# Layer 0 of a two-layer kernel: logits, dispatch, combine and first expert products as three f16 products of split halves, with a new order of steps

## The reference

```python
xn = rmsnorm(x, norm_gamma)
sn = rmsnorm(slot_embeds, slot_norm_gamma)
logits = jnp.einsum('bnd,esd->bnes', xn, sn)
dispatch = jax.nn.softmax(logits, axis=1)
combine = jax.nn.softmax(logits.reshape(b, n, e * s), axis=-1)
slots = jnp.einsum('bnd,bnes->besd', xn, dispatch)
h = jnp.einsum('besd,edh->besh', slots, w1) + b1[None, :, None, :]
h = jax.nn.gelu(h, approximate=False)
eo = jnp.einsum('besh,ehd->besd', h, w2) + b2[None, :, None, :]
out = jnp.einsum('bmd,bnm->bnd', eo, combine)
```

## Time and profile before

| | |
|---|---|
| median of 3 runs | 3189.1 us |
| lowest and highest run | 3177.04 and 3196.51 us |
| the profiled execution | 3176.99 us |
| its span, first to last instruction | 3175.3 us |
| mean granted clock of TensorE, share of full speed | 0.987 |
| PE busy in the span | 2998.4 us (94%) |
| PE weight loads | 1597.1 us (50%) |
| DVE busy | 2243.0 us (71%) |
| ACT busy | 1765.3 us (56%) |
| POOL busy | 1316.9 us (41%) |

### The profile page before, as it was taken

The page is one execution under the profiler, slowest core; times in us unless marked ns, Lnnn a source line. Parts: engine busy times, 40 slices in busy tenths (PEclk is TensorE's granted clock), DMA queues, the critical chain, the costliest instruction groups (busy, mean ns, idle before and its releaser), DMA issues.

```text
span 3175.3 us, 62002 instructions
## 1 busy us (share of the span) xinstructions
PE 2998.4 (94%) x22724; PEld 1597.1 (50%) x22724; DVE 2243.0 (71%) x4069; ACT 1765.3 (56%) x3674; POOL 1316.9 (41%) x1223
## 2 busy tenths in 40 slices
PE   4999999999999995799999999999999999999997
PEld 2565555555555553344444444444444444444443
DVE  4666666666666663787787787778778778878774
ACT  2666666665566664555555555555555555555543
POOL 1333333333333331354545545545544554455453
PEclk9999999999999998899999999999999999999998
DMA  4222222222222222434444445444444444453442
GB/s 119 51 53 51 51 51 56 64 56 63 51 51 51 62 50 83 110 100 117 128 113 123 116 115 135 111 112 126 115 121 112 128 126 104 125 135 100 124 121 67
DMA packets 271901, 297.58 MB, mean 94 GB/s; under 512 B 30832, under 2 KB 235760, under 8 KB 271088
## 3 DMA queue, kind: packets, MB, share of 16 engines
q1 hardware_dynamic: 249936, 276.88, 34.2%
q10 hardware_dynamic: 21664, 16.73, 1.7%
HBM read 141.46 MB, written 25.69 MB: 53 GB/s over the span
## 4 chain that ended last, share of the span: by engine, by line
PE 50%; DMA 3%; DVE 3%; issue 2%; SPq 2%; ACT 1%; POOL 0%; DVEq 0%; ACTq 0%; POOLq 0%
PE l_ps_out L1569 8%; PE l_ps_any L1469 6%; PE l_ps_any L1471 6%; PE l_ps_any L1470 6%; PE l_ps_any L1594 5%; PE l_ps_exp L1552 4%; PE l_ps_exp L1554 4%; PE l_ps_any L1601 4%; PE l_ps_any L1527 3%; DMA l_y_rec<-rec_scratch 2%; PE l_ps_sum L1580 2%; PE l_ps_exp L1556 2%; SPq L1099 1%; DVE l_neg_max L1392 1%; PE l_ps_any L1532 1%
## 5 line engine op out<-in xcount | busy, mean ns | idle before, releaser
L614 DVE TENSOR_REDUCE neg_max<-ps_any 128x1 f32<-128x384 f32 (+3 forms) x704 | 417.7, 636 | 264.0 <-PE ps_any L728 259.5
L1186 POOL TENSOR_TENSOR l_hid<-l_hid,l_spread 128x512 f32<-128x512 f32 x256 | 328.3, 1282 | 652.0 <-DVE l_hid L1421 481.1
L1273 ACT ACTIVATE l_probs<-l_ps_exp 128x512 f32<-128x512 f32 x640 | 376.8, 595 | 212.3 <-PE l_ps_exp L1556 201.8
L501 ACT ACTIVATE probs<-ps_exp 128x512 f32<-128x512 f32 x640 | 349.2, 602 | 151.5 <-PE ps_exp L743 150.8
L442 POOL TENSOR_SCALAR_AFFINE_SELECT probs<-probs 128x512 f32<-128x512 f32 x256 | 160.0, 637 | 591.1 <-ACT probs L501 591.1
L1392 DVE TENSOR_REDUCE l_neg_max<-l_ps_any 128x2 f32<-128x768 f32 (+2 forms) x384 | 316.3, 863 | 36.1 <-PE l_ps_any L1532 35.1
L1552 PE MATMUL l_ps_exp<-l_q_a,l_k_a 128*128 128x512 f16 (+3 forms) x1024 | 306.4, 300 | 10.0 <-DMA l_q_b<-l_max_row 6.3
L1569 PE MATMUL l_ps_out<-l_probs,l_v 128*64 128x512 f32 (+3 forms) x2048 | 303.9, 439 | 0.7 <-ACT l_yT L1248 0.7
L1425 DVE TENSOR_TENSOR l_hw<-l_hid,l_hw 128x512 f16<-128x512 f32 x272 | 258.6, 955 | 59.4 <-ACT l_hw L1256 58.9
L1554 PE MATMUL l_ps_exp<-l_q_b,l_k_b 65*128 65x512 f16 (+3 forms) x1024 | 295.3, 300 | 0.0
L1279 ACT ACTIVATE l_hid<-l_ps_any 128x512 f32<-128x512 f32 x272 | 162.4, 597 | 234.8 <-PE l_ps_any L1471 217.5
(11 more groups left out here) (233 smaller groups left out, 6514.4 us busy)
## 6 DMA issues: line engine op xcount, KB each, us to landing
l_spread<-route_scratch SPq DMA_DIRECT2D x128, 512.0 KB, 4.7
l_q_a<-l_q_hi SPq DMA_DIRECT2D x256, 128.0 KB, 2.4
l_y_rec<-rec_scratch SPq DMA_DIRECT2D x128, 256.0 KB, 4.3
l_q_b<-l_q_lo SPq DMA_DIRECT2D x128, 128.0 KB, 2.4
l_k_a<-l_k_hi SPq DMA_DIRECT2D x128, 128.0 KB, 3.0
l_k_a<-l_k_lo SPq DMA_DIRECT2D x128, 128.0 KB, 2.7
l_k_b<-l_k_hi SPq DMA_DIRECT2D x128, 128.0 KB, 2.7
q_st<-rot_hi SPq DMA_DIRECT2D x64, 128.0 KB
```

Of the source, the lines that this page charges most:

```text
L501: nc.scalar.activation(probs[:, n % 2, u], ps_exp[:, (10 * g + u) % 3], ACT.Exp, scale=float(HD0 + DR) ** -0.5).then_inc(exp_done.sem, 1)
L614: nc.vector.tensor_reduce(neg_max[:, n % 2, heads[0]:heads[0] + k, t], src, AX.X, ALU.max, negate=True).then_inc(drained["dve"], 1)
L1186: nc.gpsimd.tensor_tensor(at, at, spread[:, c % 3, n % SPREAD], ALU.mult).then_inc(weighted.sem, 1)
L1273: nc.scalar.activation(probs[:, n % 2, u], ps_exp[:, (5 * p + u) % ST_BANKS], ACT.Exp, scale=float(HD1) ** -0.5).then_inc(exp_done.sem, 1)
```

## The change

- `snT`, `xfT`, `xf` (as a new tile `xf_p`), `disp_n`/`comb_s`, `slotsT`, `w1` and `eo` become pairs of f16 halves: the high half is the value rounded to f16, the low half what is left of it. Some are scaled by powers of two (w1 by 64, shares by 1024, slots and eo by 16), and the scales are taken out again in the Gelu and in the copy of `out`.
- The products of `logits_s`, `logits_c`, `slots`, `hidden` and the four of `out` are each three f16 products, high x high, high x low and low x high, accumulated in the same bank (`split_product`). w_o's product and `expert_out` stay in float32, and so do all the turns.
- The high halves are made by ACT and the low halves by DVE, which reads the bank and the high half. For `dispatch` and `combine` every bank is now read by both, ACT first, and is free once DVE is done; the same holds for `slots` and `xfT`. `xf`'s halves are made from SBUF, ACT in the step `xf` and DVE in `xfT`. `eo` is first added into `eo_in` by DVE, then ACT makes the high half in the step `expert_out`, and DVE the low half in a new step `eo_lo`.
- w1 is loaded first on ACT's queue, in float32, into the half of `probs` that head group 1 will use, and split at the first `turn_max` by one ACT and one DVE instruction of 4096 columns; ACT waits for DVE's before the first Exp of group 1. `snT` gets its low half from DVE before DVE's first `norm`, and PE waits for it.
- `ORDER0` is another order of the same steps and `eo_lo`. The second and later `logits_s` come later in relation to the attention's groups; `attnT`, `out` and `outT` of a pass stand in the next pass; `dispatch` follows `max` 2_7; `xf` of the next pass comes after the exps of group 3 have begun, and `xfT` after the next pass's `max` 0_10; the `max` steps of the next pass's groups 0 and 1 reach further ahead.

The core of the diff:

```diff
-    ("max", 0, 1, 2), ("max", 0, 1, 3), ("max", 0, 1, 4), ("exp", 0, 0, 3), ("soft_s", 0, 0), ("exp", 0, 0, 4),
...
-    ("exp", 1, 0, 1), ("exp", 1, 0, 2), ("max", 1, 1, 1),
+    ("exp", 0, 0, 4), ("logits_s", 0, 0), ("exp", 0, 0, 5), ("exp", 0, 0, 6), ("soft_s", 0, 0),
+    ("max", 0, 1, 8), ("exp", 0, 0, 7), ("attnT", -1, 0), ("load_heads", 0, 2), ("values", 0, 0, 0),
...
+    ("outT", -1, 0), ("max", 0, 2, 5), ("max", 0, 2, 6), ("exp", 0, 1, 4), ("max", 0, 2, 7), ("dispatch", 0, 0),
+    ("dispatch", 0, 1), ("dispatch", 0, 2), ("norm", 1, 0), ("exp", 0, 1, 5), ("load_heads", 0, 3),
+    ("values", 0, 0, 2), ("out_rows", 0, 0), ("dispatch", 0, 3), ("max", 0, 2, 8), ("exp", 0, 1, 6),
+    ("max", 0, 2, 9), ("exp", 0, 1, 7), ("slots", 0, 0), ("exp", 0, 1, 8), ("logits_c", 0, 0),
+    ("logits_c", 0, 1), ("soft_c", 0, 0), ("exp", 0, 1, 9), ("turn_rows", 0, 0), ("scale", 1, 0),
+    ("max", 0, 2, 10), ("soft_c", 0, 1), ("hidden", 0, 0), ("xnT", 1, 0), ("square", 1, 0), ("values", 0, 1, 0),
+    ("turn_max", 0, 2), ("hidden", 0, 1), ("values", 0, 1, 1), ("hidden", 0, 2), ("max", 0, 3, 0),
...
+    ("soft_c", 0, 3), ("max", 0, 3, 9), ("logits_c", 0, 3), ("exp", 0, 2, 6), ("max", 0, 3, 10),
...
+    ("values", 0, 2, 0), ("r", 1, 0), ("expert_out", 0, 0), ("combine", 0, 0), ("values", 0, 2, 1),
+    ("exp", 0, 3, 0), ("exp", 0, 3, 1), ("combine", 0, 1), ("exp", 0, 3, 2), ("eo_lo", 0, 0),
+    ("values", 0, 2, 2), ("combine", 0, 2), ("out_rows", 0, 2), ("exp", 0, 3, 3), ("exp", 0, 3, 4),
...
 def by_act0(step):
 
-    name, _, n = step[:3]
-    return name in ("xnT", "xfT", "ckv", "v", "slots", "attnT", "out", "soft_s", "soft_c", "hidden", "turn_max") or (
-        name in ("dispatch", "combine") and n % 2 == 0)
+    name = step[0]
+    return name in ("xnT", "ckv", "v", "attnT", "out", "soft_s", "soft_c", "hidden", "turn_max")
...
+        w1_in = probs[:, 1, 0:E0 * HID // T].rearrange("p u t -> p (u t)").rearrange("p (e h) -> p e h", h=HID)
...
+            act.dma_start(w1_in, a["L0_ffn_w1"].rearrange("e d h -> d e h")).then_inc(w1_loaded, 16)
...
+                if name == "turn_max" and b == 0 and n == 0:
+                    act.wait_ge(w1_loaded, 16)
+                    nc.scalar.activation(w1[:, 0], w1_in, ACT.Copy, scale=W1_SCALE).then_inc(w1_hi, 1)
+                if name == "exp" and (b, n) == (0, 1) and which[1] == 0:
+                    act.wait_ge(w1_ok, 1)
...
+                if name == "expert_out":
+                    emptied(act, f"expert_out{b}")
+                    if b:
+                        filling(act, f"out{b - 1}")
+                    nc.scalar.activation(eo[:, 0].rearrange("p m d -> p (m d)"), eo_in[:], ACT.Copy, scale=EO_SCALE
+                                         ).then_inc(eo_hi.sem, 1)
...
+                    nc.scalar.activation(disp_n[:, n, 0], full(act, f"dispatch{b}_{n}"), ACT.Copy, scale=SHARE
+                                         ).then_inc(turned_hi.sem, 1)
...
+            dve.wait_ge(prep_act, 1)
+            nc.vector.tensor_tensor(snT[:, 1], ps_any[:, 0], snT[:, 0], ALU.subtract).then_inc(prep, 1)
+
+            def low_part(bank, parts, scale):
+
+                return nc.vector.scalar_tensor_tensor(out=parts[:, 1], in0=bank, scalar=scale, in1=parts[:, 0],
+                                                      op0=ALU.mult, op1=ALU.subtract)
...
+                if name == "dispatch":
+                    bank = full(dve, f"dispatch{b}_{n}")
+                    dve.wait_ge(turned_hi.sem, turned_hi.at(b, n + 1))
+                    low_part(bank, disp_n[:, n], SHARE).then_inc(drained["dve"], 1)
...
+            def split_product(out, w, x, first=True, last=True):
+
+                pe.matmul(out, w(0), x(0), start=first, stop=False)
+                pe.matmul(out, w(0), x(1), start=False, stop=False)
+                return pe.matmul(out, w(1), x(0), start=False, stop=last)
...
-                            ins = pe.matmul(out[:, c:c + S0], w1[:, e, hb * P:hb * P + P],
-                                            slotsT[:, e * S0:e * S0 + S0], start=True, stop=True)
+                            ins = split_product(out[:, c:c + S0], lambda k: w1[:, k, e, hb * P:hb * P + P],
+                                                lambda k: slotsT[:, k, e * S0:e * S0 + S0])
```

More of the change, by code:

```diff
@@ L41 @@
 RING = 4
+W1_SCALE = 64.0
+SHARE = 1024.0
+SLOT_SCALE = 16.0
+EO_SCALE = 16.0
 ST_BANKS = 2
@@ L136 @@
[L136 to L145, removed]
@@ L151 @@
[L151 to L160, removed]
@@ L163 @@
+    ("turn_max", 1, 0), ("turn_rows", 0, 3), ("max", 1, 1, 0), ("max", 1, 1, 1), ("max", 1, 1, 2),
+    ("combine", 0, 3), ("exp", 1, 0, 0), ("exp", 1, 0, 1), ("max", 1, 1, 3), ("exp", 1, 0, 2), ("max", 1, 1, 4),
+    ("max", 1, 1, 5), ("max", 1, 1, 6), ("exp", 1, 0, 3), ("max", 1, 1, 7),
 )
@@ L523, in _ @@
                         filling(act, f"out{b - 1}")
-                    copy(f"attnT{b}", attnT[:])
+                    copy(f"attnT{b}", attnT[:], SHARE * EO_SCALE)
                 if name == "out":
@@ L527, in _ @@
                         filling(act, f"outT{b - 1}")
-                    copy(f"out{b}", outT[:])
+                    copy(f"out{b}", outT[:], 1.0 / (SHARE * EO_SCALE))
                 if name == "outT":
@@ L586, in _ @@
                                                        op0=ALU.mult, op1=ALU.mult).then_inc(xf_ok.sem, 1)
+                if name == "turn_max" and b == 0 and n == 0:
+                    dve.wait_ge(w1_hi, 1)
+                    nc.vector.scalar_tensor_tensor(out=w1[:, 1], in0=w1_in, scalar=W1_SCALE, in1=w1[:, 0], op0=ALU.mult,
+                                                   op1=ALU.subtract).then_inc(w1_ok, 1)
+                if name == "xfT":
+                    dve.wait_ge(xf_hi.sem, xf_hi.at(b, 2))
+                    nc.vector.tensor_tensor(xf_p[:, 1], xf[:], xf_p[:, 0], ALU.subtract).then_inc(xf_lo.sem, 1)
+                    low_part(full(dve, f"xfT{b}"), xfT, 1.0).then_inc(drained["dve"], 1)
+                if name == "slots":
+                    bank = full(dve, f"slots{b}")
+                    dve.wait_ge(slots_hi.sem, slots_hi.at(b, 1))
+                    low_part(bank, slotsT, SLOT_SCALE / SHARE).then_inc(drained["dve"], 1)
+                if name == "eo_lo":
+                    dve.wait_ge(eo_hi.sem, eo_hi.at(b, 1))
+                    low_part(eo_in[:], eo[:].rearrange("p c m d -> p c (m d)"), EO_SCALE).then_inc(eo_ok.sem, 1)
                 if name in ("low_q", "low_k"):
@@ L667, in _ @@
             pe.wait_ge(prep_act, 1)
+            pe.wait_ge(prep, 15)
             def bank(name):
@@ L765, in _ @@
                     emptied(pe, f"xfT{b}")
-                    product(f"logits_s{b}_{n}", snT[:, n * P:n * P + P], xfT[:])
+                    split_product(bank(f"logits_s{b}_{n}"), lambda c: snT[:, c, n * P:n * P + P], xfT_part).then_inc(filled, 1)
                 if name == "logits_c":
                     emptied(pe, f"xfT{b}")
-                    product(f"logits_c{b}_{n}", xfT[:, n * P:n * P + P], snT[:])
+                    split_product(bank(f"logits_c{b}_{n}"), lambda c: xfT[:, c, n * P:n * P + P], snT_part).then_inc(filled, 1)
                 if name == "dispatch":
@@ L810, in _ @@
                     out = bank(f"out{b}")
-                    emptied(pe, f"expert_out{b}")
+                    pe.wait_ge(eo_ok.sem, eo_ok.at(b, 1))
                     for c in range(4):
                         emptied(pe, f"combine{b}_{c}")
-                        pe.matmul(out, eo[:, c], comb_s[:, c], start=(c == 0), stop=False)
+                        split_product(out, lambda k: eo[:, k, c], lambda k: comb_s[:, c, k], c == 0, False)
                     emptied(pe, f"attnT{b}")
```

104 lines of the change are left out of this document (65 added, 39 removed).

## The result

| | before | after |
|---|---|---|
| median | 3189.6 us | 3096.5 us |
| lowest to highest | 3177.0 to 3196.5 | 3095.6 to 3103.9 |
| span of the profiled execution | 3175.3 | 3094.8 |
| one pass of layer 0 | 73.9 | 68.3 |

The ratio is 0.9723 with a 95% interval of 0.9705 to 0.9741: 88 us faster by the ratio, 93 by the medians. The two profiled executions lie 80.5 us apart; that of before is the fastest of its runs. Where its other runs spend the 12 us more no trace shows. The time falls inside the range, 6.5 us above the number given.

What follows compares the result with a forecast made beforehand. PE's stream was taken to bound layer 0's sixteen passes: 7.8 us off PE less 1.5 of new waits, 16 x (7.8 - 1.5) - 8.7 = 92 us off, giving 3090 us, range 3050 to 3138.

Steps and rivals of the forecast that it cites:

- The bound is PE's stream: Layer 0's passes: PE, busy 934 of 960 us, sets their length; staying so had chance 0.70, gain 50 to 130 us.
- 3.4 us for the 16 large products: Logits, slots and out: 16 products per pass, each 0.215 us shorter on PE when split than in float32.
- 4.4 us for the small ones: Experts' first products: four `hidden` steps per pass, each 0.70 us instead of 1.79 on PE.
- the routing row: Layer 1's routing product, f16 with a 128x128 load per matmul, 0.025 us each; basis for 0.029 us in `hidden`.
- rival 3: Weight loads pace the 24 small products of a `hidden` step: 17 us slower at worst, 44 faster by half overlap; chance 0.06.
- ACT + 3.6 and DVE + 5.5 us: Added work per pass for making halves: six ACT copies of 0.60 us, eight more DVE low halves of 0.69 us.
- New waits of 1.5 us: PE's added waiting per pass, for banks emptied by two engines and full engines around `hidden`; between 0 and 4 us.
- The 1.0 us for held banks: Ten more bank fillings per pass emptied by ACT then DVE, charged at 0.10 us each.
- the 0.5 us for two full engines around `hidden`: First dispatch to last combine logits: PE down to 23.5 us, ACT up to 24.1, charged 0.5 us per pass.
- rival 4: PE waits for every turned bank: 13 us per pass, 92 us slower, deciding from 7.2 us per pass; chance 0.05.
- The start, 8.7 us: Once: 2.7 us for snT's low half before the statistics, 6 us for splitting w1; bounds 4 and 13.
- The signs: Adds 66 to 69 us apart, `hidden` 0.7, slot logits 0.215, PE above 95%, statistics near 30, then a 6 us gap.

Runs made afterwards that it cites:

- hidden_f32: The changed kernel with only the experts' first products back in float32, w1 and slotsT not split: 3145.8 us, ratio 0.9868, a pass of 71.48 us.
- bank_free: The changed kernel with dispatch and combine banks free after ACT's copy, DVE reading a tile in SBUF instead: 3097.0 us, a pass of 68.37 us.
- no_table: The changed kernel with Exp in the place of Gelu, so that two table loads per pass fall away: 3097.9 us, a pass of 68.20 us.
- old_order: The changed kernel with the order of steps of the kernel before, eo_lo put in behind group 3's third exp: 3205.7 us, ratio 1.0052.

## Why the prediction was right or wrong, point by point

- **The bound is PE's stream: right.** Work put on PE lengthens the pass by 0.7 (hidden_f32) to 1.2 times its time; the table loads taken off ACT give nothing, work taken off DVE a quarter to 0.4.
- **3.4 us for the 16 large products, 4.4 us for the small ones: right as PE time.** 0.217 and 0.029 us by the rows of after; the routing row was the right neighbour, and rival 3 is out. The Trainium skill's "TensorE: Matmul & The Clock Gate", section "LDWEIGHTS (loading the stationary operand)", gives a load as its columns over 1.2, some 107 ns for 128 columns. The trace agrees with that as a duration (0.098 us for the loads of `hidden`) and not as a pace (0.029 us).
- **ACT + 3.6 and DVE + 5.5 us: a bit high.** 48.0 and 51.0 us per pass are 1.9 and 4.1 more. Records that follow one another overlap, by 0.17 us in DVE's row of eight maxima at 68.00 us ((4.33 - 0.69)/7 = 0.52 us apart), which the sum counted twice. That could cover DVE's 1.4 us, and only a part of ACT's 1.7.
- **New waits of 1.5 us: mis-sized and put on the wrong causes.** 7.8 - 5.6 = 2.2 us (5.7 by the other reading). The 1.0 us for held banks measured nothing in bank_free, and the 0.5 us for two full engines around `hidden` nothing in no_table. The 1.0 us came from a misreading: the 10.9 and 28.3 us of the earlier trace rows are waits of PEld, and PE's own list before has nothing for the first and 5.1 us for the second. The waits that are there are others: of 3.8 us some 2.1 are y_un, the maxima and xn, each a step close behind its source. That the sum still came near with two wrong parts is luck.
- **The order taken as a thing beside the sum: the step that failed most.** The forecast moved steps at no charge and gave new waits 0 to 4 us whatever the order. With the old order they are 7.8 + 1.3 = 9.1 us per pass by the traces and some 8 by the medians, and the kernel is slower than before: the place where rival 4 decides (7.2 us) was passed, though by copies, banks and in small part DMAs together and not by the turned banks alone. The two wait lists, of before and of old_order, show that PE's float32 time had covered most of these latencies and its shorter time doesn't. The trace of before could not tell how much of it the new order would find again.
- **The start, 8.7 us: right in kind, 10.6 measured.** The statistics began at 29.57 as forecast (2.5 us later); w1's two instructions took 3.6 + 4.4 and not 4.8 + 5.5, yet some 8 us are left for them where 6 were charged. The sum had no term for the clock, and 3.9 of the 10.6 us are busy time that the lower level made longer.
- **The sum.** 16 x 6.3 - 8.7 = 92 against the 80.5 us of the profiled executions and 93 by the medians. From the traces it is 16 x 5.7 - 10.6 = 81: the sum was 12 us too high for them, and it meets the medians by the low level of the one profiled execution of before. The lower end of the range takes off 125 us, where its own terms, 16 x 7.8 - 4, give 121; nothing hangs on it.
- **The signs.** The distance of the adds (68.3), the `hidden` step (0.70 us), the slot logits (0.217 us at the upper level) and the statistics came as said. PE is busy 94.4% from 200 to 1060 us and not above 95, and the gap of 6 us behind the first `turn_max` is two waits of 3.58 and 1.26 us with a slow stretch behind them.

## What to carry to other kernels

When the bound engine gets shorter work, the order of the steps around it is part of the price: what its old length covered (copies, banks, DMAs, the longest waits 0.6 to 1.6 us each) comes out as waits, here 8 to 9 us against 7.8 won, until the steps are spread again. Change the length and the order together, and measure each alone to see which one carries the gain. A busy time of 99% in a stretch does not make an engine the bound there; take a piece of its work away and look at the length of the pass. And price a wait from the list of the engine that bounds the kernel: its weight loads wait longer and more often than it does.

## What the runs showed of the hardware

- A matmul of f16 with its own load of 128x128 weights and 64 columns goes every 0.029 us; in float32 the same product took two records at 0.112 us each. For such small products the three f16 products are 2.6 times as fast as the one in float32, for 512 columns 1.3 times.
- One instruction over 4096 columns takes 3.61 us on ACT and 4.42 us on DVE. The records of eight of 512 columns add up to 4.8 and 5.5 us, but in a row they overlap: DVE's eight maxima take 4.33 us, no longer than the one of 4096.
- A wait of PEld need not be one of PE: for the low halves of L1312, at L1469 of layer 1 before, PE waits 5.1 us, its loads 28.3.
- POOL subtracts 128x512 with an f16 result in 1.16 us, DVE in 0.69.
